# Keys from projected tokens, offsets by group and shift masks from offset limits in a deformable-attention kernel on one core

## What is computed

```
q = conv1x1(x, wq)
off = depthwise 5x5 conv of q per group, stride 4;  off /= sqrt(var + eps)
off = einsum('oi,bihw->bohw', w_off, gelu(off))          # 3 values per point
offset = stack([tanh(off[:, 0]) / 4, tanh(off[:, 1]) / 4])
dm = sigmoid(off[:, 2]);  pos = offset + ref_points
xs = grid_sample(x, pos) * dm
k, v = conv1x1(xs, wk), conv1x1(xs, wv)
attn = einsum('bcm,bcn->bmn', q, k) * scale
bias = grid_sample(rpe, (query points - pos) / 2)
attn = softmax(attn + bias);  out = conv1x1(einsum(attn, v), wo)
```

## Time and profile before

| | |
|---|---|
| median of 3 runs | 62.73 us (62.57 to 62.83) |
| the profiled execution | 62.78 us, its span 60.7 us |
| PE busy | 52.4 us, 86% of the span, 582 records |
| PE weight loads | 43.0 us, beside PE's matmuls |
| DVE busy | 37.0 us (61%), 90 instructions |
| ACT busy | 28.8 us (48%), 62 instructions |
| POOL busy | 21.5 us (35%), 45 instructions |
| zero matmuls (L655) in PE's busy time | 14.7 us, 192 records |
| chain that ended last, shares | PE 57%, DVE 11%, ACT 10%, POOL 7%, issue 5%, DMA 4% |

### The profile page before, as it was taken

How to read it: one execution, slowest core, us unless ns; L and a number is a source line. 1 busy time by engine, 2 the same in 40 slices (tenths; PEclk the granted TensorE clock), 3 DMA queues, 4 the chain that set the end, 5 groups by cost and what they waited for, 6 DMA issues and landing times.

```text
span 60.7 us, 1436 instructions
## 1 busy us (share of the span) xinstructions
PE 52.4 (86%) x582; PEld 43.0 (71%) x582; DVE 37.0 (61%) x90; ACT 28.8 (48%) x62; POOL 21.5 (35%) x45
## 2 busy tenths in 40 slices
PE   3997996998898899999999939598999998989920
PEld 3996894974587889999898929263378586778800
DVE  3368499736669899099960372479997607740320
ACT  0801051869999405007558742889437226501020
POOL 6030389793879899600420000004000591000000
PEclk9999999999999999999999999999999999999999
DMA  0699821100000000000000000000000000000004
GB/s 0 204 220 260 230 76 46 56 23 0 0 0 0 11 0 0 0 0 0 0 0 0 11 0 11 0 0 0 0 0 0 0 11 0 0 0 0 0 32 141
DMA packets 3926, 2.02 MB, mean 33 GB/s; under 512 B 2640, under 2 KB 3792, under 8 KB 3920
## 3 DMA queue, kind: packets, MB, share of 16 engines
q1 hardware_dynamic: 1424, 1.37, 7.2%
q10 hardware_dynamic: 2496, 0.57, 4.4%
HBM read 1.67 MB, written 0.26 MB: 32 GB/s over the span
## 4 chain that ended last, share of the span: by engine, by line
PE 57%; DVE 11%; ACT 10%; POOL 7%; issue 5%; DMA 4%; DVEq 0%; ACTq 0%
PE ps L655 6%; DMA x_sb<-x_rows 4%; PE ps L736 4%; ACT e_tok L610 4%; PE ps L832 3%; PE ps L729 3%; PE ps L780 3%; PE ps L801 3%; PE ps L758 3%; PE ps L871 3%; DVE taps L976 2%; POOL w_smp L473 2%; PE ps L816 2%; DVE off L978 2%; PE ps L691 2%
## 5 line engine op out<-in xcount | busy, mean ns | idle before, releaser
L655 PE MATMUL ps<-zeros 128*128 128x128 bf16 x192 | 14.7, 237 | 1.0 <-DVE zeros L953 1.0
L655 PEld LDWEIGHTS ps<-zeros 128*128 128x128 bf16 x192 | 13.4, 108 | 1.6 <-DVE zeros L953 1.0
L510 ACT ACT_TABLE_LOAD x4 | 5.1, 1283 | 1.7 <-PEq L1162 1.7
L610 ACT ACTIVATE e_tok<-ps,cst 128x1024 f32<-128x1024 f32 (+1 forms) x5 | 4.4, 941 | 1.1 <-PE ps L825 0.9
L385 POOL TENSOR_TENSOR c_scaled<-ln_c,e_sum 128x256 f32<-128x256 f32 x1 | 0.6, 620 | 11.0 <-DVE e_sum L1068 11.0
L1068 DVE TENSOR_REDUCE e_sum<-e_tok 128x4 f32<-128x1024 f32 x3 | 3.6, 1216 | 0.4 <-ACT e_tok L610 0.3
L1007 DVE COPY_PREDICATED ps<-over,ps 128x608 f32<-128x608 uint32 (+1 forms) x4 | 3.1, 777 | 0.8 <-PE ps L708 0.7
L832 PE MATMUL ps<-e_tok,t 128*32 128x256 f32 x32 | 3.1, 385 | 0.2 <-ACT e_tok L610 0.2
L708 PE MATMUL ps<-rpe_blk,minus_hat_rel 128*32 128x168 f32 x64 | 2.8, 316 | 0.5 <-DVE minus_hat_rel L1003 0.5
L496 POOL TENSOR_TENSOR o_n<-ln_c,e_rec 128x256 f32<-128x256 f32 x2 | 1.2, 620 | 5.3 <-DVE e_rec L1085 5.3
L570 ACT ACTIVATE kv<-ps,cst 128x256 f32<-128x256 f32 x4 | 1.7, 472 | 2.8 <-PE ps L729 2.8
(11 more groups left out here) (179 smaller groups left out, 124.3 us busy)
## 6 DMA issues: line engine op xcount, KB each, us to landing
w_sb<-weight ACTq DMA_DIRECT2D x1, 256.0 KB, 6.6
w_sb<-weight SPq DMA_DIRECT2D x1, 256.0 KB, 5.3
x_nat<-x_rows SPq DMA_DIRECT2D x8, 32.0 KB
wts<-weights SPq DMA_DIRECT2D x1, 192.5 KB, 4.5
cst<-shape_consts SPq DMA_DIRECT2D x1, 192.0 KB, 4.1
x_sb<-x_rows SPq DMA_DIRECT2D x1, 128.0 KB, 2.7
x_sb<-x_rows ACTq DMA_DIRECT2D x1, 128.0 KB, 2.9
cst<-shape_consts SPq DMA_DIRECT2D x1, 128.0 KB, 5.1
```

What stands on the lines that cost most here:

```text
L510: nc.scalar.add_instruction(mybir.InstLoadActFuncSet(name=nc.get_next_instruction_name(), act_func_set_id=functions, ins=[], outs=[]))
L610: return nc.scalar.activation(dst, scores, ACT.Exp, bias=const("bound"))
L655: mm(bank(n_bank, P), zeros[:, :], zeros[:, :], start=True, stop=True)
```

## The change

1. Keys. Instead of sampling tokens and projecting the samples, PE projects the tokens first: `key_tokens(h)` makes `ktok_ps[h]`, half 0 after the turned x and half 1 after the variance, ACT and DVE copy one half each to `k_tok`. For this POOL makes wk's blocks ahead of the table's, scaled by 0.5. Once w_smp is there, 32 matmuls of 32x32 sample the projected tokens into `kv_ps[0]`, pairs of images at a time in the four column groups of PE; 16 more sample `xs_ps`, now for the values alone.
2. Gate. `hat_gate` = (half_tanh + 1) times the x hats, on DVE; `w_smp` is the y hats times that. `xs` is a plain copy on ACT. The `shut` product goes, since pairs of images are told apart in `copy_heads`, which now makes four copies (head by side of the pair) for two.
3. Offsets to table rows by group: gelu, y offset, tanh, points, distances and hats are split in groups of 128 columns; the hats of group 1 move from DVE to POOL. The x offset comes after the y offsets, the gate between the rows of group 0 and group 1.
4. Masks. `over` is one comparison, on DVE, of `tx_ps` with `limits`, the values of the offset at which its tanh passes a whole column; POOL's `tx` comes later and off the masks' path.
5. Order. q is copied as soon as the taps have read it (`conv_read`); the copy `win` is ahead of the table load; `here` of group 0 moves from POOL to DVE; the logits are put together part by part for both halves at once.
6. Zero matmuls: `off_ready` 22 to 5, `off_blk_ready` 28 to 14, `w_smp_ready` 20 to 30, `xs_ready` (8) gone.

The diff, cut:

```diff
-    "xn_ready": 45, "off_ready": 22, "off_blk_ready": 28, "w_smp_ready": 20, "xs_ready": 8,
+    "xn_ready": 45, "off_ready": 5, "off_blk_ready": 14, "w_smp_ready": 30,
...
-    put("head", (p[:, None] % GC) // DH == np.arange(HG)[None, :])
+    slot = np.arange(HG * 2)[None, :]
+    put("head", ((p[:, None] % GC) // DH == slot // 2) & (p[:, None] // GC % 2 == slot % 2))
...
+    least_turn = (table_columns()[1][p // (P // NK)][:, None] - np.arange(1, MAXSHIFT + 1)[None, :]) / OFFSET
+    inside = np.clip(least_turn, -1 + 1e-9, 1 - 1e-9)
+    put("limits", np.where(np.abs(least_turn) < 1, np.arctanh(inside), np.sign(least_turn) * ALWAYS))
...
+        def hats(engine, g, k):
+            cols = slice(P * g, P * g + P)
+            return engine.tensor_scalar(minus_hat_rel[:, k, cols], a_rel[:, k, cols], -1.0, 0.0, ALU.add, ALU.min)
...
-            pool.wait_ge(txh_ready, 1)
-            link(nc.gpsimd.tensor_scalar(tx[:, :], txh[:, :], -OFFSET, const("ref_x"), ALU.mult, ALU.add))
-            for g in range(G):
-                last = nc.gpsimd.tensor_scalar(over[:, g, :], const("steps"), tx[:, g:g + 1], None, ALU.is_le)
-            link(last)
+            pool.wait_ge(over_ready, 1)
             link(nc.gpsimd.tensor_tensor(odd_over[:, :], over[:, :, 0], over[:, :, 1], ALU.subtract))
...
+            for k in range(4):
+                pool.wait_ge(a_rel_ready, 4 + k + 1)
+                hats(nc.gpsimd, 1, k).then_inc(hat_rel_ready[1], 1)
...
-            pool.wait_ge(hat_smp_ready, 1)
-            for h in range(NHALF):
-                nc.gpsimd.tensor_tensor(w_smp[:, h], hat_smp[:, h], hat_smp[:, 2], ALU.mult).then_inc(w_smp_ready, 1)
...
+            pool.wait_ge(hat_gate_ready, 1)
+            for h in range(NHALF):
+                nc.gpsimd.tensor_tensor(w_smp[:, h], hat_smp[:, h], hat_gate[:, :], ALU.mult).then_inc(w_smp_ready, 1)
...
+            act.wait_ge(ktok_done, 1)
+            nc.scalar.activation(k_tok[:, 0], ktok_ps[0], ACT.Copy).then_inc(ktok_copied, 1)
...
                 for hh in range(HG):
-                    nc.scalar.activation(kv[:, w, :, :, hh], kv_ps[w].rearrange("p g (t j) -> p g t j", t=NT), ACT.Copy,
-                                         scale=const("head")[:, hh:hh + 1]).then_inc(ready, 1)
+                    for side in range(2):
+                        nc.scalar.activation(pairs_sb[:, :, hh, :, side], pairs_ps[:, :, :, side], ACT.Copy,
+                                             scale=const("head")[:, 2 * hh + side:2 * hh + side + 1]).then_inc(ready, 1)
...
+            def key_tokens(h):
+
+                for gi in range(G):
+                    last = mm(ktok_ps[h][:, gi].rearrange("p g o -> p (g o)"), xn[:, gi, h * P:(h + 1) * P],
+                              wblk[:, 1, gi].rearrange("p g b o -> p (g b o)"), start=True, stop=True)
+                last.then_inc(ktok_done, 1)
...
+            for h in range(NHALF):
+                pe.wait_ge(w_smp_ready, h + 1)
+                for gi in range(G):
+                    for g in range(G):
+                        for j in range(4):
+                            rows = slice(32 * j, 32 * j + 32)
+                            last = mm(kv_ps[0][rows, g, rows], k_tok[:, h, gi, g, rows],
+                                      w_smp[:, h, P * gi + 32 * j:P * gi + 32 * j + 32],
+                                      start=False, stop=(h == NHALF - 1 and gi == G - 1), skip_group_check=True)
+            last.then_inc(k_done, 1)
...
+            for g in range(G):
+                dve.wait_ge(tanh_y_ready, g + 1)
+                place(0, g, 1).then_inc(points_y_ready, 1)
+            dve.wait_ge(turn_done, 1)
+            tt(over[:, :, :], tx_ps.unsqueeze(2).to_broadcast([P, G, MAXSHIFT]),
+               const("limits").unsqueeze(1).to_broadcast([P, G, MAXSHIFT]), ALU.is_le).then_inc(over_ready, 1)
```

More of the change, by code:

```diff
@@ L50 @@
 SQRT_SET, LN_EXP_SET, GELU_SET = 3, 6, 10
-SHUT = 2.0 ** 40
+ALWAYS = 3e38
 def columns(*widths):
@@ L434, in _ @@
             pool.wait_ge(weights_loaded[1], 16)
+            link(nc.gpsimd.tensor_scalar(wk_s[:, :, :], wkvo[:, 0], 0.5 * QK_SCALE, None, ALU.mult))
+            for g in range(G):
+                blocks(wblk[:, 1, g], wk_s[:, g].rearrange("p (g o) -> p g o", g=G), G, GC).then_inc(wk_ready, 1)
             pool.wait_ge(const_loaded[2], 16)
@@ L700, in _ @@
-            offset(2, start=False).then_inc(off_done, 1)
+            last.then_inc(turn_done, 1)
+            pe.wait_ge(q_copied, G)
+            offset(off_x_ps, 1, cols.rearrange("p g n -> p (g n)")).then_inc(off_x_done, 1)
             pe.wait_ge(rpe_blk_ready, 1)
-            pe.wait_ge(q_copied, G)
+            pe.wait_ge(tanh_y_ready, G)
             for g in range(G):
+                if g == 1:
+                    offset(off_gate_ps, 2, cols.rearrange("p g n -> p (g n)")).then_inc(off_gate_done, 1)
+                    pe.wait_ge(tanh_x_ready, 1)
@@ L992, in _, with place @@
                 in1=wkvo[:, 2], op0=ALU.mult, op1=ALU.add).then_inc(wo_c_ready, 1)
-            for axis in range(2):
-                dve.wait_ge(tanh_ready, axis + 1)
-                stt(out=points[:, axis].rearrange("p (q n) -> p q n", n=N),
-                    in0=th[:, axis].rearrange("p (q n) -> p q n", n=N), scalar=OFFSET,
-                    in1=const("points")[:, axis * N:(axis + 1) * N].unsqueeze(1).to_broadcast([P, G * B, N]),
-                    op0=ALU.mult, op1=ALU.add).then_inc(points_ready, 1)
+            dve.wait_ge(ktok_done, 2)
+            nc.vector.tensor_copy(k_tok[:, 1], ktok_ps[1]).then_inc(ktok_copied, 1)
+            def place(axis, first, groups):
+                cols = slice(P * first, P * first + P * groups)
+                return stt(out=points[:, axis, cols].rearrange("p (q n) -> p q n", n=N),
+                           in0=th[:, axis, cols].rearrange("p (q n) -> p q n", n=N), scalar=OFFSET,
+                           in1=const("points")[:, axis * N:(axis + 1) * N].unsqueeze(1).to_broadcast(
+                               [P, groups * B, N]), op0=ALU.mult, op1=ALU.add)
+            for g in range(G):
+                dve.wait_ge(tanh_y_ready, g + 1)
[3 more added lines that the diff above has]
+               const("limits").unsqueeze(1).to_broadcast([P, G, MAXSHIFT]), ALU.is_le).then_inc(over_ready, 1)
             for k in range(4):
                 dve.wait_ge(a_rel_ready, k + 1)
-                ts(minus_hat_rel[:, k], a_rel[:, k], -1.0, 0.0, ALU.add, ALU.min).then_inc(hat_rel_ready, 1)
+                hats(nc.vector, 0, k).then_inc(hat_rel_ready[0], 1)
+            dve.wait_ge(tanh_x_ready, 1)
+            place(1, 0, G).then_inc(points_x_ready, 1)
             def shifted(g, width, mask, by):
```

191 lines of the change are left out of this document (111 added, 80 removed).

## The result

The changed kernel takes 65.39 us (65.22 to 65.64, 4 runs) against 62.69 (62.57 to 62.83) before, a ratio of 1.041 (95% interval 1.037 to 1.045). It is slower by 2.7 us; the forecast was 65.1, within 63.8 to 66.9. Its profiled execution took 65.29 us with a span of 63.1, where before it was 62.78 and 60.7. One run of a later experiment (e4, 66.48 us, mean granted clock 0.974 of full) fell in a slower state that can befall any kernel, and its numbers leave that run out.

What follows compares the result with a forecast made beforehand. It took the kernel to be bound by a chain of waits over four engines to 22.9 us, then PE to 34; late keys and jointly announced logits, less front gains, summed to +2.33 us on 62.78: 65.1 us, range 63.8 to 66.9.

Steps and rivals of the forecast that it cites:

- Start: Up to the gate's table load: no cost, bounds 0 and +0.3 us; key-token copy ends at 10.04.
- cover: At the start, 0.07 us between the key-token copy's end (10.04) and off_sq (10.11); if gone, all that follows is late.
- Front: From gelu to table rows: 0.55 us earlier, shifts starting at 16.69, with the point waiting for POOL's gate_blk.
- Masks and hats: Masks leave the chain; POOL's group 1 hats, 0.45 us each, hide inside group 0's shifts: nothing, upper bound +0.45.
- Gate: hat_gate stands on DVE behind five shifts, 20.57 to 21.00; w_smp ends at 22.49, where it was 19.88.
- the largest term: Logits announced with both halves at the end: half 0 reaches DVE at 28.18 instead of 25.74, 2.44 us later.
- Keys: Last small matmuls end at 23.08, four copies take 1.14 us; k ready at 24.26 instead of 23.75, 0.5 late.
- Logits: From 24.30 PE needs 3.90 us with both halves in the last set; half 0 is seen at 28.18, 2.44 later.
- After it: Behind the maximum: value copies seen at 31.34, probability transposes at 33.26 instead of 30.93; from there as before.
- B: Rival: longer PE idle gaps drop the granted clock to 1.2 GHz in the logits, 67 to 69 us; chance 0.09.
- C: Rival: the front wins, faster, if k is ready before 21.97; shifts at 14.0 would give 62.4 us; chance 0.07.
- D: Rival: the late half is hidden and only PE's queue counts, 63.8 us, slower all the same; chance 0.04.

Runs made afterwards that it cites:

- e4: The changed kernel with the four hats of group 1 on DVE instead of POOL: 64.71 us, ratio 1.027 to the kernel before.
- the repeat: The changed kernel run once more, unchanged, as yardstick for the runs beside it: 65.57 us.
- e1: The changed kernel with its logits put together half by half again: 64.63 us, ratio 1.028 to the kernel before.
- e3: The changed kernel with two head copies of 256 columns for four of 128, masks by side left out (results wrong): 65.15 us, ratio 1.036.
- e5: The changed kernel with group 1's hats on DVE and hat_gate ahead of group 1's three shifts: 63.55 us, ratio 1.013 to the kernel before.
- e6: e5 with the logits half by half and `left` of group 0 ahead of PE's wait for the keys: 62.80 us, ratio 1.000.
- e7: e6 with both key-token products behind the variance, both copied by DVE, and wo's sum behind the taps: 62.65 us, ratio 0.997.
- e2: The kernel before with only its logits' order changed, to both halves jointly: 63.80 us beside 62.89, ratio 1.015.

## Why the prediction was right

The median is 0.3 us above the point; against the profiled execution, on which the sum was made, it is 0.2 (65.29 for 65.1), with +2.60 at the transposes for +2.33. Its mechanism was right in the main, and the closeness of the number is partly luck. The first of DVE's taps (before, changed, repeat) is the last common event ahead of the change:

```profile
6.96 0.77 DVE L976 TENSOR_TENSOR taps<-ps,wts 128x100 f32<-128x100 f32 x4 [0.96 <-PE ps L665]
```

```profile
6.80 0.77 DVE L1034 TENSOR_TENSOR taps<-ps,wts 128x100 f32<-128x100 f32 x4 [0.96 <-PE ps L699]
```

```profile
7.51 0.77 DVE L1034 TENSOR_TENSOR taps<-ps,wts 128x100 f32<-128x100 f32 x4 [1.45 <-PE ps L699]
```

Counted from it, the transposes come 2.76 us later than before (26.73 for 23.97), and 2.57 in the repeat. The 0.16 by which the taps began earlier in this execution, and the 0.16 that the steps behind the transposes took less, were not in the forecast and brought the time nearer to it; some 0.1 to 0.2 more outside the span worked the other way.

- **Start.** Put at nothing, with a cover of 0.07 us. The cover was used up: wk's blocks stood at 8.44 and the token copy ended at 10.26, for 8.3 and 10.04. From the taps to off_sq it took 3.36 us for 3.15 before. That is a cost of 0.21, of which the start of off_sq (10.16 for 10.11) shows only 0.05 because the taps began earlier. In the repeat, e1, e3, e5 and e6 it was 3.15 and cost nothing; in e4 it was 3.63, a cost of 0.48 and beyond the bound of 0.3. It goes with the landing of wk's weights: POOL's wk_s, which waits for them, starts 0.02 ahead of the taps in the changed kernel, 0.25 behind them in e4, and 0.24 or more ahead of them where it cost nothing.
- **Front.** The rows started at 14.85 (forecast 14.97) and the first shift at 16.35 (16.69). Two sizes were off. The point was not held up: it took 0.31 us from 13.71, beside gate_blk's last 0.15, where I had it wait and end at 14.14. And from the start of the rows to the shift it was 1.50 us, not 1.72. What failed was the term that took the point as blocked until gate_blk's end (13.86). The Trainium skill, "SBUF — State Buffer", section "Who interferes with whom", calls the shared ports an exclusive lock; in this overlap the trace doesn't show one, since the point took its usual time. For long overlaps the traces agree that the two contend: off_wblk took 0.80 beside POOL's block products here, and 0.42 in the repeat with nothing of POOL's beside it. In e7 it took 0.44 although POOL's copy of 128 columns ran beside its first 0.28 us.
- **Masks and hats.** POOL's tensor_scalar of 128 columns took 0.64, not 0.45; I took the nearer row by width and not by cost. Group 1's shifts began at 19.16 instead of 18.95, a wait of 0.45 for PE that the forecast lacked. What I missed entirely is that the hats push POOL's taps to 21.28, so that by the chain w_smp would have been late even with an early gate (not run). In the changed kernel the two paths end 0.08 apart, and e4 gains 0.26 where only DVE's is left.
- **Gate.** hat_gate at 20.78 for 20.57, directly behind the fifth shift as forecast; w_smp's end 22.70 for 22.49. e5 shows that this wait, with the hats, is worth 1.4 us in the trace, more than the logits' order, which the forecast called the largest term. Part of what it counted there was the lateness of the keys.
- **Keys.** The last 16 small products ended 0.56 us after w_smp (22.71 to 23.27), for 0.46 and 0.13 in the forecast; the copies took 1.14, the forecast to the hundredth; q·k started at 24.48 for 24.30. The floor of 25 ns between starts in the Trainium skill, "TensorE: Matmul & The Clock Gate", section "Wait — 56ns, not 53.3ns?", would by an estimate make 0.8 us of the 32; the 32 records of L777 took 0.49, so the trace disagrees and the row was the better guide.
- **Logits.** The maximum came at 28.48 for 28.18, 4.00 us after q·k instead of 3.88. e1 and e2 show the joint halves alone at 0.8 to 1.0 us at the values. Of the 2.74 us by which the maximum came late, e2 shows 1.29 for the joint order; q·k began 0.46 late (24.48 for 24.02), and two turned sets of some 0.43 each, which PE made ahead of q·k before, now stand behind it. By this estimate that is 2.6 together.
- **After it.** Values at 31.64 for 31.34 and transposes at 33.53 for 33.26: the same 0.30 late, as it came in.
- **Rivals.** B: PE idled 1.07 and 1.20 us, longer than the 0.92 of before, and the granted clock stayed at 2.4 GHz. C: k was ready at 24.43, where it had to be by 21.97; the front gained 0.89 but none of it reached the keys. D: vo did wait for ACT.

## What to carry to other kernels

Work that is taken off a chain gains nothing if its successor stands in a queue behind longer work: here a product of 0.42 us behind five shifts, and taps behind hats, held an engine that had been freed. Before moving a step to a less busy engine, list what already stands there and who waits for it, and look for a second path that ends within some tenths of the first, since the chain names only one. And where two halves feed the next engine, let the first be finished first: announcing both at the end cost 0.8 to 1.0 us with no instruction added. Last, compare traces from a common event, and look at the time outside the span too: here each held some tenths that would have been credited to an edit.

## What the runs showed of the hardware

- A tensor_scalar of 128 fp32 columns takes 0.64 us on GpSimd, as much as its product of 256 columns (0.63); on VectorE the hats of group 0 take 0.23, as the groups by line and form of the changed kernel show (busy us, mean ns). A product's cost per column is no guide to a tensor_scalar's.

```profile
L395 POOL TENSOR_SCALAR minus_hat_rel<-a_rel 128x128 f32<-128x128 f32 x4 | 2.5, 647 | 1.0 <-ACT a_rel L567 1.0
...
L395 DVE TENSOR_SCALAR minus_hat_rel<-a_rel 128x128 f32<-128x128 f32 x4 | 0.9, 228 | 0.4 <-ACT a_rel L567 0.2
```

- An instruction's duration changes with what runs beside it, and that moves with the order. These are timings side by side; no run isolates the cause. GpSimd's `right` took 1.64 us beside VectorE's last tap, whose two inputs are in SBUF, and its next two products 1.18 together; in e5 that tap ran later, `right` took 1.21 and the products 1.64. None of these was waited for; only the 0.21 that `tap_here` lost beside hat_gate lay on the chain.
- 32 matmul records rotating over the four column groups (L777) end in 0.49 us with their latency; the 32 records of another product, all into one group, took 1.19.
- The start of the work moves from run to run: the taps began between 6.64 us (e4) and 7.51 (the repeat) in the profiled executions, and with one front they were 7.84 or 7.85 us ahead of the table rows unless the token copy held up off_sq (8.05 in the changed kernel, 8.31 in e4).
- The time outside the span differs by kernel: about 2.2 us with the hats on GpSimd, 1.8 to 1.9 in the kernels from e4 on, 2.0 to 2.1 in the kernel before. The cause is open.
